# PV products of two neighbouring slots in one burst, with the score lag at two slots, in a fused attention and mixture-of-experts layer

## What is computed

```python
x = x + attention(layernorm(x))      # 16 heads, causal, softmax
x = x + shared(layernorm(x)) + sum_e comb[:, e] * expert_e(layernorm(x))
# per head
logits = where(causal, q @ k.T / 8, -large)
probs = softmax(logits)
attn = probs @ v                     # the PV products
```

## Time and profile before

| what | us |
|---|---|
| median of 3 runs | 1104.42 (1104.1 to 1106.73) |
| the profiled execution, its own time | 1103.3 |
| its span, first to last instruction | 1101.5 |
| TensorE busy | 1062.1 (96%) |
| VectorE, ScalarE, GpSimd busy | 800.2, 785.8, 757.1 |
| first scores of head 0 | at 60.4 |
| last PV product of head 15 | at about 818 |

### The profile page before, as it was taken

One profiled execution on the slowest core, in us unless ns is written; L12 is line 12 of the kernel. 1 busy time (PEld: TensorE's weight loads), 2 busy tenths in 40 slices (PEclk: granted clock), 3 DMA queues, 4 the chain that ended last, 5 costly groups with the idle time before them and its releaser, 6 DMA issues.

```text
span 1101.5 us, 25737 instructions
## 1 busy us (share of the span) xinstructions
PE 1062.1 (96%) x10580; PEld 871.4 (79%) x10580; DVE 800.2 (73%) x1659; ACT 785.8 (71%) x952; POOL 757.1 (69%) x427
## 2 busy tenths in 40 slices
PE   7899999999999999999999999999976999999998
PEld 5578888888888888888888888888855677777776
DVE  5966878787787878778786877878225477777765
ACT  3068777878878787887888788788963566666664
POOL 3058878878887887887888788788970555555540
PEclk8679999999999999999999999999986999999999
DMA  2330312303032130303213030221100222111001
GB/s 81 68 78 3 77 32 55 79 2 85 12 69 51 35 79 2 85 12 68 53 34 79 1 85 21 59 54 27 45 1 1 81 80 80 60 60 60 39 1 38
DMA packets 24653, 53.22 MB, mean 48 GB/s; under 512 B 5720, under 2 KB 8024, under 8 KB 22488
## 3 DMA queue, kind: packets, MB, share of 16 engines
q1 hardware_dynamic: 24544, 51.68, 18.3%
HBM read 16.86 MB, written 1.11 MB: 16 GB/s over the span
## 4 chain that ended last, share of the span: by engine, by line
PE 72%; POOL 11%; issue 6%; DVE 5%; DMA 4%; ACT 1%; SPq 0%; POOLq 0%; ACTq 0%; DVEq 0%
PE bg L793 13%; PE st L825 12%; PE st L826 12%; PE pv L850 6%; PE pv L852 6%; PE pv L854 6%; POOL xw L442 4%; POOL p_lo L420 3%; DMA attn<-comb_dram 3%; PE bg L743 3%; PE bg L783 2%; POOL k_lohi L447 2%; PE bg L744 2%; PE bg L745 2%; POOL q_lo_shift L434 2%
## 5 line engine op out<-in xcount | busy, mean ns | idle before, releaser
L420 POOL TENSOR_TENSOR p_lo<-prob,p_hi 128x1024 f16<-128x1024 f32 x320 | 617.5, 1948 | 164.1 <-ACT p_hi L504 162.3
L503 ACT ACTIVATE prob<-st,p_bias 128x1024 f32<-128x1024 f32 x320 | 330.0, 1031 | 132.6 <-PE st L826 99.7
L504 ACT ACTIVATE p_hi<-st,p_bias 128x1024 f16<-128x1024 f32 x320 | 327.9, 1025 | 0.0
L632 DVE TENSOR_REDUCE row_max<-bg 128x1 f32<-128x512 f32 x384 | 255.6, 686 | 16.8 <-PE bg L793 11.5
L825 PE MATMUL st<-q_hihi,k_lohi 128*128 128x512 f32 (+1 forms) x640 | 253.3, 396 | 1.9 <-ACT p_hi L504 1.1
L850 PEld LDWEIGHTS pv<-v_parts,p_hi 128*128 128x128 f16 x2176 | 197.6, 96 | 60.2 <-issue 37.6
L793 PE MATMUL bg<-k_lohi,q_hihi 128*128 128x512 f32 (+3 forms) x640 | 240.7, 408 | 2.6 <-DVE v_parts L622 2.1
L826 PE MATMUL st<-q_lo_shift,k_hi_one 65*128 65x512 f32 (+1 forms) x640 | 239.9, 375 | 0.0
L850 PE MATMUL pv<-v_parts,p_hi 128*128 128x65 f16 x2176 | 236.2, 194 | 2.1 <-POOL p_lo L420 2.1
L852 PE MATMUL pv<-v_parts,p_hi 128*128 128x64 f16 x2176 | 233.7, 195 | 0.0
L854 PE MATMUL pv<-v_parts,p_lo 128*128 128x65 f16 x2176 | 232.0, 192 | 0.0
(11 more groups left out here) (147 smaller groups left out, 1645.7 us busy)
## 6 DMA issues: line engine op xcount, KB each, us to landing
q_hihi<-k_lohi SPq DMA_DIRECT2D x128, 128.0 KB, 2.3
k_lohi<-q_lo_shift SPq DMA_DIRECT2D x64, 128.0 KB, 2.3
k_hi_one<-k_lohi SPq DMA_DIRECT2D x16, 512.0 KB, 4.3
attn<-comb_dram SPq DMA_DIRECT2D x8, 1024.0 KB, 4.8
e_raw<-ffn_w SPq DMA_DIRECT2D x9, 576.0 KB, 5.5
w_raw<-qkv_w SPq DMA_DIRECT2D x8, 192.0 KB, 2.3
res<-x_t SPq DMA_DIRECT2D x4, 256.0 KB, 4.0
out_t<-xn SPq DMA_DIRECT2D x4, 256.0 KB, 2.6
```

Of the source, the lines that this page charges most:

```text
L420: nc.gpsimd.tensor_tensor(o, a, b, ALU.subtract).then_inc(p_lo_ready, 1)
L503: nc.scalar.activation(o32, src, ACT.Exp, bias=p_bias[:], scale=D ** -0.5)
L504: nc.scalar.activation(o16, src, ACT.Exp, bias=p_bias[:], scale=D ** -0.5).then_inc(exp_done, 1)
L632: nc.vector.tensor_reduce(row_max[:, t, c:c + 1], bank, AX_X, ALU.max).then_inc(bg_drained, 1)
```

## The change

LAG is 2, and PV is issued in odd slots only: at the end of odd slot n the PV products of slots n - 3 and n - 2, one after the other. In slot 1 these are slots 18 and 19 of the head before. Even slots have scores and background tasks alone. At the end of the last head slots 18 and 19 follow. The scores and the rule for placing tasks around them stay; the planner's reserve for `normalise` moves with LAG, from slots 3, 5, 9, 15 to 2, 4, 8, 14, and with it the slots of some `max` tasks. `normalise` of slot m is VectorE's first work in slot m + 3 in place of m + 4. The set of matmuls, transfers and operations is the same.

```diff
-LAG = 3
+LAG = 2
...
                     scores(h, n, 1)
                     for task in SLOTS[h][n][2:]:
                         background_task(task)
-                    m = (n - LAG) % NG
-                    if m < n or h:
-                        for k in range(2):
-                            p_times_v(h if m < n else h - 1, m, k)
+                    if n % 2 and (n > LAG or h):
+                        for m in (n - 1 - LAG, n - LAG):
+                            for k in range(2):
+                                p_times_v(h if m >= 0 else h - 1, m % NG, k)
             for n in range(NG - LAG, NG):
                 for k in range(2):
                     p_times_v(H - 1, n, k)
```

## The result

The changed kernel took 1126.71 us (median of 4 runs, 1123.27 to 1129.1) against 1105.58 for the kernel before beside it (1104.1 to 1106.82): a ratio of 1.0189, 95% interval 1.017 to 1.0207. It is slower by some 21 us; forecast were +18.5 and a time of 1123, range 1104 to 1132.

What follows compares the result with a forecast made beforehand. TensorE's own instruction stream was taken to bound the first fifteen heads. The terms -12 + 21 + 6 + 3.5 gave +18.5 us: 1121.8 against the profiled execution, 1123 as the median, range 1104 to 1132.

Steps and rivals of the forecast that it cites:

- Switches, -12: TensorE, first fifteen heads: ten fewer switches from PV to fp32 matmuls a head save 0.8 us a head, 12 us.
- Rival (e): The switch from PV costs nothing, so nothing is saved and the waits stay: 1135 us; chance 0.03.
- Background banks, +21: First fifteen heads: background tasks come closer together, so TensorE waits for VectorE to drain three banks; 21 us lost.
- The walk: Step-by-step timing of slots 10 and 11 of head 9: 0.45 us lost to waits, 0.09 saved; then extended to other pairs.
- some 15 us: Sign in the trace: TensorE's matmuls and weight loads at L793 wait this long in all for VectorE's row_max.
- p_lo, +6: PV of slot 17 in even heads waits for GpSimd's p_lo, about 0.8 us in each of eight heads: 6 us.
- Last head, +3.5: Last head: scores stand behind PV, so GpSimd's p_lo run gets gaps; 4.3 us, 3.5 after some is absorbed by backlog.
- The cycle of 4.4 us: Last head: time from the end of p_lo(n-2) until p_lo(n+1) can start, through PV, scores and exp.
- (a): The waits do not appear and the switches go: 1092 us; chance 0.09.
- (b): Waits and switches cancel: bank waits half the forecast, none for GpSimd, 2 us in the last head; 1104 us; chance 0.07.
- (c): Small idle gaps lower TensorE's granted clock for some 10 us a head: 5 us a head, 1198 us; chance 0.03.
- (d): VectorE's backlog passes from pair to pair of slots: +30 to +40 us, 1139 us; chance 0.06.

Runs made afterwards that it cites:

- Light row maxima: Changed kernel with VectorE reducing only half the columns of each max task, exp scale set to 0.01; 1107.29 us, ratio 1.0023.
- light GpSimd: Changed kernel with GpSimd computing p_lo for only half the columns of each key tile, zero in the rest; 1115.09 us, ratio 1.0067.
- late merge: Kernel before with LAG still 3 and PV of slots n-4 and n-3 issued together at the end of even slot n; 1114.95 us, ratio 1.0098.
- both feeders light: VectorE's max tasks and GpSimd's p_lo both cut to half the columns: 1093.86 us in the kernel before, 1094.94 in the changed one.

## Why the prediction was right

**Switches, -12.** The step of 0.32 against 0.23 is real and is saved where nothing else waits (0.08 to 0.10 in slots 2 and 3, and in no head less). The whole of 12 us is inferred: no run shows it free of waits. Rival (e), that a switch is free, falls with the saving, and so does, for this kernel, the reading of the Trainium skill's rule ("TensorE: Matmul & The Clock Gate", "Step-by-step: what each phase is for") that the next tile's weights load while this tile's matmul runs. Behind PV products that start 0.03 us apart the trace does not agree: the first fp32 matmul takes 0.09 us longer.

**Background banks, +21.** The mechanism was right and its size nearly so. The walk gave the pair of slots 10 and 11 to 0.02 us. Light row maxima took 13.5 us out of the stage and left the waits behind att_t and v. The waits that the trace would show, "some 15 us" behind row_max at L793, are 14.9 at the loads; the 12.5 behind att_lo and v_parts were not in that figure. The split by heads was off: odd heads were to lose more. By the heads' lengths odd ones lost 1.1 to 1.15 net (2.0 - 0.8 = 1.2 forecast), even ones 1.35 (0.95 - 0.8 + 0.8 = 0.95 forecast). Of the even heads' excess at most 0.1 is p_lo; the term of 0.95 for their banks should have been some 1.3. Lengths of pairs of slots must be compared with care here, since PV of other slots now falls into a pair: slots 4 and 5 of head 8 took 5.52 us where they took 4.74, but 15 more products of 0.031 us explain 0.47 of that. With such products taken out, the even heads' losses are largest in slots 10 and 11 (0.45), then in 6-7 and 12-13 (0.2 each, after the saving).

**p_lo, +6.** Right in place (PV of slot 17 in even heads) and size (0.73 against 0.8 each; 7.0 us in all from the run with a light GpSimd).

**Last head, +3.5.** 3.9 measured, and gone in the late merge (+0.4). The gaps of GpSimd are two long ones (1.36 and 1.09) and three of 0.4 to 0.6, where three of 1.1 and five of 0.2 were drawn; that the sum fits is in part luck. The step that holds is that scores stand behind a PV burst. That GpSimd must be the full engine does not: with both feeders light the merge cost the last head 3.4 us all the same, at ScalarE, one piece of it by the clock. The cycle of 4.4 us also left out the last head's att_t and att_y.

**The other rivals.** (a) and (b) needed the waits to be absent or half; they are there. (c), the clock, did not move: from 67 to 837 us of the changed kernel the granted clock is 1.00. So small idles between groups of matmuls did not make it swing in the changed kernel, as the Trainium skill describes for another one ("TensorE: Matmul & The Clock Gate", "A second HAM failure mode: psum-queue depth-cycling"). In the last head of three other runs (the lag alone, GpSimd light, both light and merged) it did fall once, for some 3 us, and what sets it off there is open. The 10 us a head in the price of (c) are in no run. (d), backlog carried on from pair to pair, did not show: VectorE was idle 1.04 us before the pair that was looked at. Put together, the 17.2 us net of the fifteen heads (15 forecast) are -12 for the switches and 7.0 for p_lo, which leaves 22 for the banks with their exposed loads; 21 were forecast. That 22 is a remainder and rests on the inferred 12.

## What to carry to other kernels

In a kernel whose main engine is busy all the time, ask of a reordering not only what it saves there but how far apart it leaves the requests to the others: here a burst that seemed to be just work was the pause in which a ring of three banks emptied. Work that is cheap on the main engine and dear on its consumer has to stay interleaved with work that needs no consumer. And where a change comes with a parameter (here the lag), run each alone: the lag by itself cost 34 us, more than both together. And before a slow feeder is blamed, make it light in both kernels: the last head's loss stayed and moved to the next engine.

## What the runs showed that I had not expected

That merging softens the shorter lag: +34 us with single slots, +21 with bursts, and +11 for bursts without it, of which half was one badly placed task a head (+4 with it moved). And that 13 us hung on where the planner put a reserve of 0.6 us: in the merged kernel four entries of a list of costs were worth as much as the 12 us expected of all ten switches a head.
